# Twelve elementwise operations per attention step move to GpSimd, rescalings of PSUM banks to VectorE, casts to ScalarE

## The reference, cut to what matters

```python
w = (qw.astype(jnp.float32) - ZERO) * jnp.repeat(scales, GS, axis=0)     # GS = 128 rows share a scale
q = dequant_matmul(hidden, qw_q, scales_q)      # 32 heads of 128
k = dequant_matmul(hidden, qw_k, scales_k)      # 8 heads, each for 4 query heads
v = dequant_matmul(hidden, qw_v, scales_v)
q, k = apply_rope(q, cos, sin), apply_rope(k, cos, sin)   # x * cos + rotate_half(x) * sin
scores = jnp.where(causal, q @ k.T / sqrt(128), min)
ctx = softmax(scores) @ v
x = x + dequant_matmul(ctx, qw_o, scales_o)
```

## Time and profile before

| | us |
|---|---|
| median of 3 runs | 1920.22 (1913.91 to 1923.56) |
| the profiled execution, its own time | 1917.04 |
| its span in the trace | 1915.0 |
| PE busy, share of the span | 1722.9, 90% |
| DVE busy | 1585.7, 83% |
| ACT busy | 1394.6, 73% |
| POOL busy | 55.6, 3% |

### The profile page before, as it was taken

The page is one execution under the profiler, slowest core; times in us unless marked ns, Lnnn a source line. Parts: engine busy times, 40 slices in busy tenths (PEclk is TensorE's granted clock), DMA queues, the critical chain, the costliest instruction groups (busy, mean ns, idle before and its releaser), DMA issues. The chain is left out here.

```text
span 1915.0 us, 38654 instructions
## 1 busy us (share of the span) xinstructions
PE 1722.9 (90%) x14306; PEld 942.5 (49%) x14306; DVE 1585.7 (83%) x2670; ACT 1394.6 (73%) x2361; POOL 55.6 (3%) x50
## 2 busy tenths in 40 slices
PE   3689999998999999999989999999999777779999
PEld 3435555544454455445545544454555455554444
DVE  6598999998999899989998998989998868992222
ACT  2568888988888888888888988888988527960000
POOL 0200000000000000000000000000000001320000
PEclk8799999999999999999999999999999978999999
DMA  7321111020103010200111020103020230111111
GB/s 212 100 78 35 34 46 46 1 69 12 46 1 78 4 45 19 61 25 24 34 47 46 2 75 6 46 1 78 12 58 11 89 110 23 40 40 45 44 44 44
DMA packets 118063, 87.67 MB, mean 46 GB/s; under 512 B 13404, under 2 KB 108004, under 8 KB 117860
## 3 DMA queue, kind: packets, MB, share of 16 engines
q1 hardware_dynamic: 117220, 84.83, 15.0%
q10 hardware_dynamic: 640, 0.13, 0.0%
HBM read 76.55 MB, written 8.39 MB: 44 GB/s over the span
## 5 line engine op out<-in xcount | busy, mean ns | idle before, releaser
L1182 ACT ACTIVATE pj<-pj,ratio 128x512 f32<-128x512 f32 x865 | 576.4, 685 | 108.1 <-PE pj L1437 102.3
L1435 PE MATMUL pj<-hid,wts 128*128 128x512 f16 x1024 | 392.1, 383 | 67.1 <-DVE pj L804 25.0
L1437 PE MATMUL pj<-hid,wts 128*128 128x512 f16 x1024 | 390.3, 381 | 0.0
L1191 ACT ACTIVATE sbk<-sbk,wts 128x512 f32<-128x512 f32 x384 | 262.4, 683 | 41.5 <-PE sbk L1504 36.6
L1191 ACT ACTIVATE sa<-sa,wts 128x512 f32<-128x512 f32 x384 | 261.1, 680 | 24.1 <-PE sa L1504 23.9
L1435 PEld LDWEIGHTS pj<-hid,wts 128*128 128x128 f16 x1024 | 99.8, 97 | 237.2 <-ACT pj L1182 72.7
L1447 PEld LDWEIGHTS tp<-wts,hid 128*128 128x128 f16 x3072 | 181.7, 98 | 32.5 <-issue 3.5
L1447 PE MATMUL tp<-wts,hid 128*128 128x128 f16 x3072 | 192.5, 219 | 0.5
L1437 PEld LDWEIGHTS pj<-hid,wts 128*128 128x128 f16 x1024 | 100.6, 98 | 76.6 <-issue 1.1
L704 DVE SCALAR_TENSOR_TENSOR work<-pj,ratio,cos_t 128x512 f32<-128x512 f32 x128 | 95.5, 746 | 45.0 <-PE pj L1437 35.8
L1182 ACT ACTIVATE ex<-ex,ratio 128x512 f32<-128x512 f32 x193 | 128.1, 664 | 3.8 <-PE ex L1437 1.2
(11 more groups left out here) (243 smaller groups left out, 3184.5 us busy)
## 6 DMA issues: line engine op xcount, KB each, us to landing
wts<-qo_d SPq DMA_DIRECT2D x64, 256.0 KB, 3.2
y<-x_d SPq DMA_DIRECT2D x7, 2048.0 KB, 7.9
wts<-qq_d SPq DMA_DIRECT2D x35, 256.0 KB, 3.1
int_even<-qq_d SPq DMA_DIRECT2D x29, 256.0 KB, 2.9
out_d<-y SPq DMA_DIRECT2D x12, 512.0 KB, 2.6
work<-qv_d SPq DMA_DIRECT2D x16, 256.0 KB, 7.5
work<-sv_d SPq DMA_DIRECT2D x16, 256.0 KB, 9.5
work<-wb_d SPq DMA_DIRECT2D x8, 512.0 KB, 4.4
```

The lines of the kernel that those rows point to most:

```text
L1182: act.activation(unit_bank[u][:, :], unit_bank[u][:, :], ACT.Copy, scale=ratio[:, KT * u + j:KT * u + j + 1]).then_inc(u_scaled[u], 1)
L1191: act.activation(out_bank[t % 2][:, :], out_bank[t % 2][:, :], ACT.Copy, scale=o_ratio[:, REP * t + h:REP * t + h + 1]).then_inc(o_scaled[ ...
L1435: mm(bank[:, :], w_int[:, u, j, :], hid[:, 0, j, CH * c:CH * (c + 1)], start=j == 0, stop=False, skip_group_check=True)
L1437: mm(bank[:, :], w_int[:, u, j, :], hid[:, 1, j, CH * c:CH * (c + 1)], start=False, stop=True, skip_group_check=True).then_inc(u_done[u], 1)
```

## The change

Twelve operations per step go from DVE to a GpSimd stream of its own: the five `rope_add`, the `rope_split` of the units 2, 3 and 4, both `soft_shift` and both `prob_split`. They wait for and raise the same semaphores as before. `rope_high` (all five units) and `prob_high` (both halves) are on ACT; before, ACT had one of each. DVE keeps `rope_split` of the units 0 and 1.

Twelve rescalings go from ACT to DVE: `rescale` (2,1), (1,1), (1,2), (0,6), (2,3) and `rescale_out` (0,1), (1,2), (5,1), (4,2), (5,2), (7,1), (7,2). Two go the other way: `rescale` (2,2) and (3,0). All four lists are written in a new order: on PE scores(1) has 28 quanta of its step ahead of it, where there were 16, transpose_probs(0) 43 (32), transpose_probs(1) 56 (51); tile 7 of the out projection ends ahead of tile 6. GpSimd's maximum of the base weights (its operation for L1030) moves behind the last step, since it stands behind the new stream in the program.

```diff
@@ gpsimd
+            def rope_add(p4, u):
+                gp.wait_ge(S["u_read"], steps(p4, NU, u + 1))
+                gp.tensor_tensor(ra[:, u % 2, :], ra[:, u % 2, :], rb[:, :], ALU.add).then_inc(S["rope_sum"], 1)
+
+            def rope_split(p4, u):
+                gp.wait_ge(rope_hi[u], steps(p4, 1, 1))
+                gp.tensor_tensor(rope_write(u, 1), rope_sum_of(u), rope_write(u, 0), ALU.subtract).then_inc(qk_ready[u], 1)
+
+            def soft_shift(p4, h):
+                gp.wait_ge(S["rowmaxed"], steps(p4, 2, h + 1))
...
+            def prob_split(p4, h):
+                gp.wait_ge(S["probs_hi"], steps(p4, 2, h + 1))
...
+            def step(p4, ahead):
+
+                rope_add(p4, 4)
+                soft_shift(p4, 0)
+                rope_split(p4, 4)
+                if ahead:
+                    rope_add(ahead, 0)
+                soft_shift(p4, 1)
+                prob_split(p4, 0)
+                if ahead:
+                    rope_add(ahead, 1)
+                prob_split(p4, 1)
+                if ahead:
+                    rope_add(ahead, 2)
+                    rope_add(ahead, 3)
+                    rope_split(ahead, 2)
+                    rope_split(ahead, 3)
...
+            step((0, 0), (0, 1))
+            with gp.Fori(1, NC * NKV - 1) as s:
+                step((s, 0), (s, 1))
+            step((0, NC * NKV - 1), None)
             over_partitions("stat_wb", 1, T_WB, T_WB + 1, "top_wb")
@@ vector, step
                 soft_norm(p4, 1)
                 pt_copy(p4, 0)
-                if ahead:
-                    rescale(ahead, 3, 0)
-                    rope_add(ahead, 0)
-                    rope_cos(ahead, 1)
...
+                if out4:
+                    rescale_out(out4, 5, 1)
                 if ahead:
                     rope_split(ahead, 0)
...
@@ scalar, step
                 exps(p4, 0)
...
+                rope_high(p4, 4)
...
+                prob_high(p4, 0)
+                if ahead:
+                    rope_high(ahead, 0)
```

More of the change, by code:

```diff
@@ L924, in step @@
                     add_out(out4, 7)
+                    between("out", 6)
+                    add_out(out4, 6)
                     between("out", 7)
-                if ahead:
-                    rope_split(ahead, 3)
                 pieces(3)
@@ L1556, in step @@
                 if ahead:
-                    quantum(ahead, 0, 4)
-                scores(p4, 1)
-                if ahead:
+                    quantum(ahead, 1, 2)
                     quantum(ahead, 2, 2)
@@ L1573, in step @@
                 if ahead:
-                    quantum(ahead, 1, 3)
-                if out4:
-                    out_quantum(out4, 3, 0)
-                if ahead:
+                    quantum(ahead, 1, 4)
                     quantum(ahead, 0, 7)
                 if out4:
+                    out_quantum(out4, 3, 1)
+                scores(p4, 1)
+                if ahead:
+                    quantum(ahead, 1, 5)
+                if out4:
+                    out_quantum(out4, 3, 2)
                     out_quantum(out4, 2, 2)
@@ L1601, in step @@
+                if ahead:
                     quantum(ahead, 2, 5)
+                    quantum(ahead, 3, 2)
+                transpose_probs(p4, 0)
                 if out4:
                     out_quantum(out4, 4, 1)
-                    out_quantum(out4, 3, 3)
-                    after(3)
+                    out_quantum(out4, 5, 1)
                 if ahead:
-                    quantum(ahead, 3, 2)
+                    quantum(ahead, 4, 0)
+                    quantum(ahead, 3, 3)
+                    quantum(ahead, 2, 6)
@@ L1629, in step @@
                 if ahead:
-                    quantum(ahead, 4, 1)
                     quantum(ahead, 3, 5)
@@ L1645, in step @@
                 weigh_values(p4, 1)
+                if ahead:
+                    quantum(ahead, 3, 7)
+                if out4:
+                    out_quantum(out4, 7, 2)
+                if ahead:
+                    quantum(ahead, 4, 4)
                 if out4:
```

285 lines of the change are left out of this document (122 added, 163 removed).

## The result

The changed kernel takes **1988.3 us** (median of four runs, 1986.8 to 1990.0) against 1921.9 us (1913.9 to 1923.9) for the kernel before on the same chip: 1.035 times as long, 95% interval 1.033 to 1.037. The forecast was 1890 us, with a chance of 0.17 for slower. The profiled execution has a span of 1987.2 us, the one of before 1915.0.

What follows compares the result with a forecast made beforehand. PE nearly bounds the short step, in-order DVE work lengthens the others. Per pass 6.0 - 2.3 - 0.7 = 3.0 us, over 7.75 passes 23, with the first step 27: 1917 - 27 = 1890 us, range 1850 to 1940.

Steps and rivals of the forecast that it cites:

- The sum of a pass: Four attention-loop steps: 6.0 us relief minus 2.3 for collisions and 0.7 for hops, 3.0 us less.
- The relief: Less DVE work shortens the three long steps by 1.8 us each, the short one by 0.6: 6.0 us per pass.
- The price of DVE time, 0.78: In the long attention steps, 1 us of DVE work costs 0.78 us of step, from comparing third and second steps.
- 2.3 us less DVE work a step: DVE per step: 8.9 us of operations and casts go, 6.6 us of rescalings come.
- Collisions, 2.3 us a pass: GpSimd holding up DVE operations with SBUF inputs: at most 4.6 us per pass, half of it taken.
- rival 2: Shared port: every DVE-GpSimd meeting costs its 0.84 us, 4.6 per pass; 1908 us, about no change; chance 0.20.
- sure half: The 2.3 us of collisions counted as certain, laid to soft_norm's last multiplication on DVE meeting GpSimd.
- Rescalings as 0.66 us of DVE time: Ten more rescalings on DVE, 0.66 us each back to back, add 6.6 us of DVE work per step.
- High halves on ACT: ACT loses 10 rescalings and gains 5 casts, 3.7 us less per step; nothing counted for it.
- New hops: PE waits 0.5 to 1.0 us at weigh_values(0), an earlier 0.8 us wait goes; 0.7 us lost per pass.
- First step: Step 0, without out projection: DVE has 6.9 us less, 5.4 at 0.78; 4 us shorter taken.
- The third: Rival: second softmax half becomes the path, PE stands at transposes(1); 1946 us, chance 0.17 together with the fourth rival.

Runs made afterwards that it cites:

- e11: Changed kernel with three rescalings, rescale(0, 6) and the two of output column 7, given back from DVE to ACT; 1951.0 us, ratio 1.017.
- e15: Changed kernel with those three rescalings back on ACT and GpSimd's operations cut to one eighth of their columns or less, except in the first step; 1915.7 us, ratio 0.999.
- e1: Changed kernel with GpSimd's rope sums, low halves and shifts cut to one eighth of their columns or less, except in the first step; 1953.0 us, ratio 1.017.
- e3: Kernel before with its weight pieces cut to 8 columns on DVE; 1907.5 us, ratio 0.993.
- e9: Kernel before with only the twelve operations per step moved to GpSimd; high halves stay on DVE, rescalings and orders as before; 1904.7 us, ratio 0.993.
- e12: Changed kernel with six of the twelve rescalings per step on DVE given back to ACT; 1963.4 us, ratio 1.023.
- e2: Changed kernel with each of the 18 weight pieces of a pass cut to 8 columns on DVE; 1985.3 us, ratio 1.034.
- e13: Kernel before with the twelve operations on GpSimd and the high halves on ACT, rescalings and other orders as before; 1970.1 us, ratio 1.027.
- e5: Changed kernel with each weight piece replaced by a DVE reduction of about the same length; 1976.6 us, ratio 1.031.

## Why the prediction was wrong, point by point

**The sum of a pass.** The forecast was 3.0 us less; by the table it is 8.4 us more. Two steps of the prediction failed, and a third was undersized. The ten additional rescalings stand in it as DVE load and as nothing else; three of them cost 5.0 us a pass (after against e11). The relief was priced at 6.0 us; with both costs taken away (e15) the pass is 1.0 us shorter than before. And GpSimd's operations cost 4.6 us (after against e1) instead of 2.3. The first alone turns the sign of the sum.

**The price of DVE time, 0.78: failed.** I took it from two steps of the same kernel: the third is 3.1 us longer than the second with 4.0 us more DVE work. But the same rows have PE busy 42.48 against 40.36 us, with 357 matmuls against 347. A step's program has the same matmuls each time (the four rows have 353 on the mean): the step is cut at DVE's v_split, and the third row has taken in some of a neighbour's. So 2.1 of the 3.1 us are PE at work, and only 1.0 is more idle time. Taking DVE work away shows what it is worth over a pass: 0.47 by the pieces (e3), 0.08 by the twelve operations (e9). PE is idle 1.5 to 2.5 us in the first three steps of the earlier trace rows, so there was little to buy. The relief of 6.0 us a pass had at most about 4 us behind it at e3's price, and under 1 at that of e9.

**2.3 us less DVE work a step.** Right in the second step (2.0 less, and 41.3 us as forecast). In the first and third DVE's busy time rose by 2.0 and 1.2, which is the sign of being wrong that the prediction names. In a pass DVE has 0.4 us more instead of 9.2 less; 7.7 us of that go with the length of GpSimd's operations (e1).

**Collisions, 2.3 us a pass: undersized.** GpSimd's length costs 4.6 (after against e1), as much as the most that I had worked out, and rival 2's price. That the two numbers agree is luck: the 4.6 of e1 has GpSimd's place in the chain in it, and the 5.9 us of held-up DVE time that I had were 8.8. That the pieces collide was the open question, and they do: 1.13 to 1.47 us, as "what would show it" asked. The scale operations I had not counted at all. And the "sure half", soft_norm's multiplication, isn't there: in the groups 1 to 6 none is held up.

```profile
L796 DVE SCALAR_TENSOR_TENSOR work<-work,rinv x64: 691/692/1208, 131.0 to 1578.6; 128x512 f32<-128x512 f32 x64
```

**Rescalings as 0.66 us of DVE time: the step that gave the sign.** This left out what they are: a hand-over that PE waits for. "Ten more of 0.75" stands in the sum as load alone, and their waits as nothing, but three of them cost 35 us (e11). Load does not explain it, since taking more of it away gave nothing (e12) or little (e2); the waits at rescale(0, 6) and add_out(6) show them late, or making others late, in DVE's queue. With the three on ACT, PE waits 1.1 to 1.9 us a step for ACT's rescalings (e11), and the kernel is faster all the same.

**GpSimd, 12.6 us a step.** It is 14.1 to 14.6. A sum takes 1.28 us; the 1.05 came from a multiplication whose second operand is one column per 64. f16, the open point, made it no slower.

**High halves on ACT: "I count nothing".** In the orders of before, with the twelve operations on GpSimd, they cost 65 us (e13). What they cost in the changed kernel's orders was not tried alone.

**New hops.** The wait at weigh_values(0) came as worked out: 0.5 us in the first two steps, 2.0 in the third; none shows in the fourth. But the 0.8 us at a rescaling on DVE, which was to go, only fell to 0.5 in the first three steps, at another rescaling (L831). The low halves of unit 4 had the room that I gave them: PE doesn't wait for them in the changed kernel.

**First step.** Forecast 4 us shorter, it is 4.3 longer (42.0 us). With GpSimd's part alone it is 37.2 (e9), with the highs on ACT 39.3 (e13). The hops that I noted in half a sentence seem to be the larger term; no run tries them alone. The sums and casts ahead of the first step pass ACT and GpSimd too, which I had not looked at: the first v_split starts at 121.6 to 124.0 us in all kernels that have this, and at 118.1 to 119.9 in those that have the start of before.

**GpSimd's maxima.** Nothing was counted, and behind the last v_split there are 2.0 us more, within what the runs scatter there (425.7 to 430.9).

**The rivals.** The third had the sign and less than half of the size (1946, 29 us more, where it is 72), and not the place: it put the wait at transposes(1), and PE waits at add_out(6) and at rescalings. Rival 2 had the size of GpSimd's part, and would have been no change on the whole. None of the four had a rescaling that is late on DVE.

## What to carry to other kernels

What an engine's time is worth is measured by taking some away, or worked out from the bound engine's idle time; two steps of different content don't give it, above all when their edges are marked by the engine that lags. Before moving an operation, ask who waits for it and what stands ahead of it in its new queue: here three such operations of 0.7 us cost 35 us in a queue that was late, while twelve given to an idle engine brought 14. A helper whose operations hold up those of its neighbour paid only while the neighbour had room (e9); so move fewer things, and leave the hand-overs where they are.

## What the runs showed of the hardware

- An operation of 8 columns on DVE is held up as long as one of 512 by GpSimd (0.16 to 1.23 us in e2, 0.41 to 1.47 in the changed kernel). It ends 0.03 us after GpSimd's, one of 512 columns 0.28. Small scale operations pay the same (128x32: 0.19 to 1.09 us).
- A reduction on DVE (0.452 to 0.470 us in e5) is not held up beside the same GpSimd operations that hold a piece up to 1.47 us.
- GpSimd takes, for 128x512 on the mean, 1.28 us with two operands of f32, 1.16 to 1.18 with one of f32 and one of f16, 1.09 with a second operand that is one column per 64. f16 made it no slower.
- Behind 4.2 us in which PE stood, its granted clock was at the lower level for 3.4 us (0.51), and eight matmuls took 1.7 us more.
